# Value folds on quarters of the array, another order of GpSimd's splits, an unrolled quantised layer and another order of the third attention

## The reference

```python
# L0, L3: 16 heads of 64 columns
attn = softmax(mask(q @ k.T * scale))          # per head
out  = (attn @ v).reshape(b, n, INNER) @ Wo + bo
# L0 feed-forward: fake quantisation, one scale for the whole tensor
xq   = fake_quant(x)                           # needs max|x| of all blocks
h    = silu(xq @ q(w_gate).T) * (xq @ q(w_up).T)
y    = fake_quant(h) @ q(w_down).T             # needs max|h| of all blocks
# L2: one head of 256 columns, rows masked
out  = (softmax(where(mask, q @ k.T / 16, -1e10)) @ v) @ Wfc + bfc
# layers L1 to L3 follow it with mixtures of 8 experts
```

## Time and profile before

| what | value |
|---|---|
| median of 3 runs | 825.51 us (824.89 to 826.6) |
| profiled execution, own time | 823.46 us |
| its span in the trace | 821.7 us |
| mean granted clock of PE | 0.969 |
| busy share: PE, DVE, ACT, POOL | 91%, 69%, 53%, 42% |
| chain that ended last: PE, DVE, ACT, POOL | 59%, 9%, 8%, 8% |

### The profile page before, as it was taken

One profiled execution on the slowest core, in us unless ns is written; L12 is line 12 of the kernel. 1 busy time (PEld: TensorE's weight loads), 2 busy tenths in 40 slices (PEclk: granted clock), 3 DMA queues, 4 the chain that ended last, 5 costly groups with the idle time before them and its releaser, 6 DMA issues.

```text
span 821.7 us, 14453 instructions
## 1 busy us (share of the span) xinstructions
PE 750.0 (91%) x4384; PEld 604.9 (74%) x4384; DVE 568.0 (69%) x1647; ACT 438.5 (53%) x1182; POOL 348.2 (42%) x343
## 2 busy tenths in 40 slices
PE   6999989987799889799998879989999989899996
PEld 5677878863367666589996867756888876599984
DVE  3788878777988576657754878775667666855525
ACT  2477978857763753145553544445565244245542
POOL 1016998941301567614554011346541434324550
PEclk9999999997989978899999999999999999999999
DMA  8629970060001002248527400001000141334328
GB/s 275 102 91 345 327 244 1 1 205 0 1 1 39 2 20 89 100 126 269 161 85 259 132 0 2 2 0 39 1 1 1 51 151 56 104 111 149 123 85 307
DMA packets 55610, 83.38 MB, mean 101 GB/s; under 512 B 14816, under 2 KB 44512, under 8 KB 55264
## 3 DMA queue, kind: packets, MB, share of 16 engines
q1 hardware_dynamic: 48624, 63.52, 25.0%
q0 software_dynamic: 6912, 18.95, 6.4%
HBM read 61.41 MB, written 37.95 MB: 121 GB/s over the span
## 4 chain that ended last, share of the span: by engine, by line
PE 59%; DVE 9%; ACT 8%; POOL 8%; issue 6%; DMA 5%; DVEq 2%; POOLq 2%; SPq 1%; ACTq 0%
PE sh L848 16%; PE ob L848 13%; PE sh L1312 6%; PE ob L1312 6%; PE pt L805 6%; POOL xg L693 4%; PE pt L848 2%; POOL wA L630 2%; PE sh L1331 2%; PE pt L1304 2%; DMA work<-xg 2%; PE ob L1463 2%; DMA area<-yt 2%; ACT work L1560 1%; PE ob L1130 1%
## 5 line engine op out<-in xcount | busy, mean ns | idle before, releaser
L848 PE MATMUL ob<-area,work 128*128 128x256 f32 x512 | 116.1, 380 | 3.1 <-ACT work L1537 2.1
L702 POOL DMA_INDIRECT yt<-xn,work x72 | 69.3, 963 | 100.6 <-ACT xn L1872 86.1
L848 PEld LDWEIGHTS ob<-area,work 128*128 128x128 f32 x512 | 96.4, 190 | 19.8 <-issue 5.7
L607 POOL TENSOR_TENSOR rstd<-var,minush 128x4 f32<-128x4 f32 (+1 forms) x29 | 30.9, 1066 | 173.2 <-DVE var L2029 163.4
L1560 ACT ACTIVATE work<-work,mx 128x64 f32<-128x64 f32 x256 | 85.2, 335 | 19.4 <-DVE mx L2155 19.4
L693 POOL DMA_INDIRECT xg<-area,dest x64 | 63.5, 991 | 45.2 <-DVE dest L2492 27.5
L805 PE MATMUL pt<-ident,work 128*128 128x128 f32 (+1 forms) x292 | 41.4, 282 | 16.7 <-DMA cols<-in_L_xattn_ln_c_b 5.3
L805 PEld LDWEIGHTS pt<-ident,work 128*128 128x128 f32 (+1 forms) x292 | 33.4, 141 | 24.1 <-issue 14.3
L1537 ACT COPY work<-pt 128x512 f32<-128x512 f32 (+1 forms) x74 | 39.9, 582 | 17.7 <-PE pt L805 17.6
L848 PE MATMUL ob<-area 128*128 128x256 f32 (+1 forms) x152 | 40.2, 419 | 9.2 <-DVE x L2079 5.4
L1560 ACT ACTIVATION_READ_ACCUMULATOR work<-work,mx 128x1 f32 x256 | 48.1, 188 | 0.0
(11 more groups left out here) (364 smaller groups left out, 1933.9 us busy)
## 6 DMA issues: line engine op xcount, KB each, us to landing
work<-xg SPq DMA_DIRECT2D x80, 129.0 KB, 2.3
area<-in_L_ffn_w SPq DMA_DIRECT2D x4, 2048.0 KB, 10.9
area<-yt SPq DMA_DIRECT2D x16, 512.0 KB, 7.5
area<-in_L_xattn_Wq SPq DMA_DIRECT2D x2, 1024.0 KB, 10.1
x<-in_x SPq DMA_DIRECT2D x1, 2048.0 KB, 16.0
area<-in_L_xattn_Wo SPq DMA_DIRECT2D x2, 1024.0 KB, 11.5
area<-in_L_xattn_Wkv SPq DMA_DIRECT2D x2, 1024.0 KB, 6.3
out<-x SPq DMA_DIRECT2D x4, 512.0 KB, 4.4
```

Source lines behind the costliest of these rows:

```text
L607: pool.tensor_tensor(rstd[:, n], var[:, n], minush[:, n], ALU.pow).then_inc(given, 1)
L702: pool.indirect_dma_start(yt[:, :], bass.IndirectOffsetOnAxis(ap=back_to[:, 2 * i + q:2 * i + q + 1], axis=0), ypair[i][:, q * D:(q + 1) * ...
L848: mm = pe.matmul(o, a, b, start=(k == 0), stop=(k == len(lhs) - 1))
```

## The change

Four parts, in one kernel.

**A. Value folds.** The padded `vD16` and `vD6` become plain `vT16` and `vT6`: one copy of 512 columns takes the place of two of 64 rows, the clearing goes (two on DVE, one of 4096 columns on POOL in stage 4). `quarters` forms a step from eight matmuls of 64 rows and 64 columns: rows half `j` of the stationary, output partitions `64 * ((j + b) % 2)`, odd and even `b` in the two halves of `sh`. Both `j` of a `b` write the same columns of `sh` on different partitions. The keys' copies exchange the heads of a pair for odd batches to match. On DVE the first normalisation moves from after step 0 to after step 5, the bias from after step 3 to after step 7 (`bias_added`, for which PE waits before the first product with values), the statistics of block 3 into the attention. In stages 4 and 5 the fold units are dealt out anew, so that all eight value steps end in stage 4.

**B. Splits.** POOL does the split of `x` for block 2 behind the keys of block 2, ahead of the norm factors and the keys of block 3.

**C. Quantised layer.** The loop is written out. Gate and up of block 0 are interleaved with the transposes of blocks 2 and 3; twelve matmuls on `sh1` (`warm`) follow `largest`; the silu's table is loaded earlier; transposes 2 and 3 are moved by DVE after its groups 0 and 1; clearing and scales move ahead on DVE.

**D. Third attention.** DVE's order of `shift`, `norm1`, `combine` and `finish` changes, and `combine(3, 3)` is done in two parts; PE transposes the norm of the next block after the products with values, ACT moves it after the next block's exponentials.

```diff
+            def quarters(o, vT, w, m, b):
+
+                for j in range(2):
+                    r, to = slice(64 * j, 64 * j + 64), 64 * ((j + b) % 2)
+                    mm = pe.matmul(o[to:to + 64, b // 2 * D:(b // 2 + 1) * D], vT[r, m * NC_ + b * C:m * NC_ + (b + 1) * C],
+                                   w[r, m * D:(m + 1) * D], start=True, stop=True)
+                return mm
...
-                        mm = pe.matmul(sh[n % 2][:, b * D:(b + 1) * D], vD16[:, m, b, :, :].rearrange("p j c -> p (j c)"),
-                                       wo16[:, m * D:(m + 1) * D], start=True, stop=True)
+                        mm = quarters(sh[n % 2][:, b % 2 * 512:(b % 2 + 1) * 512], vT16, wo16, m, b)
...
-                        for j in range(2):
-                            ins = dve.tensor_copy(vD16[64 * j:64 * j + 64, 4 * e - 6:4 * e - 4, :, j, :],
-                                                  src[64 * j:64 * j + 64, :].rearrange("p (m b c) -> p m b c", m=2, b=NB))
-                        ins.then_inc(sh_taken, 1)
+                        dve.tensor_copy(vT16[:, (e - 2) * 1024 + 512:(e - 1) * 1024], src).then_inc(sh_taken, 1)
...
-                       12: lambda: normalise0(0), 13: lambda: first_stats(straight[2]), 14: lambda: norm0(1),
-                       15: values_bias, 16: lambda: first_stats(straight[3])})
+                       13: lambda: first_stats(straight[2]), 14: lambda: norm0(1),
+                       17: lambda: normalise0(0), 19: values_bias})
...
-        stage5_folds = ((26, 28, 30), (30, 34, 36), (36, 40, 42), (42, 44, 44))
+        stage4_folds = ((14, 16, 18), (18, 20, 22), (22, 24, 26), (26, 28, 28))
+        stage5_folds = ((28, 30, 32), (32, 34, 36), (36, 40, 42), (42, 44, 44))
...
             split_keys(2)
+            split_x(2)
+            block_rstd(NB - 1, NB - 1)
             split_keys(3)
...
+            warm(sh[1], 12)
...
+            turn(0)
+            turn(1)
+            pe.wait_ge(pt_moved, first_turn + 1)
+            gate_up(straight[0], 0)
+            turn(2)
+            gate_up(straight[0], 1)
+            turn(3)
+            gate_up(straight[0], 2)
+            pe.wait_ge(pt_moved, first_turn + NB)
+            for u in range(3, NB * NFQ):
+                gate_up(straight[u // NFQ], u % NFQ)
...
+                    combine(3, straight[-1], (0,))
+                    norm1(stage, straight[1])
+                    shift(straight[1])
+                    combine(3, straight[-1], (1,))
+                    shift(straight[2])
+                    norm1(stage, straight[2])
+                    finish(straight[0])
+                    shift(straight[3])
+                    finish(straight[1])
+                    norm1(stage, straight[3])
+                    finish(straight[2])
```

More of the change, by code:

```diff
@@ L1008, in fold_units @@
             def fold_units(first, last):
-                for u in range(first, min(last, KEYS6)):
+                for u in range(first, min(last, VALS6)):
                     o = sh[1][:, (u % 2) * 512:(u % 2 + 1) * 512]
@@ L1033, in fold_units @@
                             mm = pe.transpose(o[:, q * P:(q + 1) * P], wq16[:, at:at + P], ident[:, :])
-                    else:
-                        m, half = (u - 12) // 2, u % 2
-                        for q in range(2):
-                            mm = pe.matmul(o[:, q * D:(q + 1) * D], vD6[:, m, 2 * half + q, :, :].rearrange("p j c -> p (j c)"),
-                                           wo6[:, m * D:(m + 1) * D], start=True, stop=True)
-                    mm.then_inc(f_full, 1)
+                    mm.then_inc(f_full, 1)
+                for u in range(max(first, VALS6), min(last, KEYS6), 2):
+                    m = (u - VALS6) // 2
+                    pe.wait_ge(f_taken, u)
+                    if m == 0:
+                        pe.wait_ge(in_wo, 32)
+                    for b in range(NB):
+                        mm = quarters(sh[1][:, b % 2 * 512:(b % 2 + 1) * 512], vT6, wo6, m, b)
+                        if b >= 2:
+                            mm.then_inc(f_full, 1)
                 for u in range(max(first, KEYS6), last, 2):
@@ L1111, in attend1 @@
                             scores(straight[b.u + 1])
-                        norm_T1(stage, straight[b.u + 1])
+                        else:
+                            norm_T1(stage, straight[b.u + 1])
                     elif stage == 2:
@@ L1133, in attend1 @@
                         mm.then_inc(o_full, 1)
+                    if stage == 4 and b.u + 1 < NB:
+                        norm_T1(stage, straight[b.u + 1])
                     if stage == 2 and b.u == NB - 1:
@@ L1424, in _, with turn @@
             largest(0)
-            for b in range(NB):
+            warm(sh[1], 12)
+            first_turn = n
+            def turn(b):
+                n = first_turn + b
                 pe.wait_ge(x_int, b + 1)
@@ L1935, in gate_silu @@
                     if f in BY_POOL:
[L1936 removed]
+                        act.activation(hall[:, f, b.u * S:(b.u + 1) * S], gu[slot][1], ACT.Copy,
                                        scale=qw[:, 2, f:f + 1]).then_inc(gu_out, 1)
[L1938 removed]
+            for b in straight:
+                gate_silu(b)
             n = start_of("pt", 2) - 6
@@ L2085, in fold16 @@
                 g = gates[:, 0:1]
-                def off_diagonal(j):
-                    dve.memset(vD16[64 * j:64 * j + 64, :, :, 1 - j, :], 0.0)
-                if stage == 0:
-                    for j in range(2):
-                        off_diagonal(j)
                 for e in range(4):
@@ L2504, in bias_part, with combine @@
                 dve.tensor_copy(part, row).then_inc(bias_split, 1)
-            def combine(stage, b):
-                for h in range(2):
+            def combine(stage, b, parts=(0, 1)):
+                for h in parts:
                     dve.wait_ge(y_in[2 * b.u + h], 16 if stage == 3 else 32)
@@ new lines, in _ @@
+            for n in range(NB * NFQ):
+                b, f = straight[n // NFQ], n % NFQ
+                r = RFQ if f == NFQ - 1 else P
+                if f in BY_DVE:
+                    dve.wait_ge(act_done[1], b.scaled(NFQ, f + 1))
+                    dve.scalar_tensor_tensor(hall[0:r, f, b.u * S:(b.u + 1) * S], gu[n % 4][1][0:r, :],
+                                             qw[0:r, 2, f:f + 1], gate_t[n % 4][0:r, :],
+                                             ALU.mult, ALU.mult).then_inc(gu_half, 1)
+                if n in (0, 1):
+                    xq_move(2 + n)
+                if n >= 2 and n % 2 == 0:
+                    magnitude(n - 2)
```

183 lines of the change are left out of this document (72 added, 111 removed).

## The result

The changed kernel takes 816.85 us (median of 4 runs, 813.8 to 818.14), the kernel before beside it 826.06 (824.89 to 827.09): ratio 0.989, 95% interval 0.9861 to 0.9918. The forecast was 814 with a range of 809 to 820.5.

The account below looks back on a forecast made before the run. PE sets most of the end, but in the touched stretches others feed it, often DVE. Gains 5.3 + 1.0 + 2.0 + 2.4 + 1.0 = 11.7 off 823.46 give 811.8, on the median 814 us; range 809 to 820.5.

Parts of the forecast that it names:

- Value steps: Stage 0: quarter steps of 0.88 us, DVE stays the slow engine, scores start sooner; gain 5.3 us.
- The first rival: Value steps: quarters run two at a time, a step takes 1.75 us; 818.8 us on the median, chance 0.25.
- The fourth rival: Value steps: quarters do not run side by side, a step takes 3.5 us; slower at 835.3 us, chance 0.04.
- The second rival: PE's clock falls in the thinner value steps, half the scores run at half clock; 1.8 lost, 815.5 us, chance 0.10.
- First attention: Stage 0 attention: PE's 1.93 wait for POOL's split goes, moved statistics cost some; gain 1.0 us.
- Quantised layer: Third group's product comes sooner, DVE's 25.4 us behind it unchanged; gain 2.0, between 0.8 at half clock and 3.6.
- Third attention: DVE's new order removes idle times of 6.5 us and adds two waits totalling 4.15; gain 2.4 us.
- The walk along the waits: Third attention: following PE's work in the new order to find when DVE's two shifts can start; new waits 1.3 and 2.85.
- its waits of 1.3 and 2.85: Third attention: new DVE waits ahead of `shift` of block 2 (1.3 us) and of block 3 (2.85 us).
- the third rival: Third attention: DVE's new waits are as long as the old, 2.4 less gain; 816.2 us, chance 0.08.
- L2's experts: Stage 5: block 1's chain waits for two moves, 1.05 us, instead of four, 2.03; gain 1.0 us.
- The sum 11.7: Whole kernel: the five gains 5.3, 1.0, 2.0, 2.4 and 1.0 us added, taken off the profiled 823.46 us.

Follow-up runs that it names:

- the run with the clock held: Changed kernel, new third-attention order kept, plus matmuls that nothing reads on PE in that stage's waits: 814.61 us, ratio 0.9865.

## Why the prediction was right, and where it was wrong

**Value steps: right, to 0.1 us.** Steps of 0.88 were taken, 0.98 measured; DVE stayed the slow engine, and the four things taken off it add up (5.3 forecast, 5.22 measured), but for one wait of 0.56 for PE that the prediction had at nothing and some small gains that make up for it. The first rival, quarters in pairs, is out: a step would take 1.75. The Trainium skill, page "TensorEngine Tiling (Array Packing)", section "Restrictions and Gotchas", which stood behind that rival, does not agree with this trace if read as a rule that makes row halves wait: both row halves of a batch write one `sh` half on different partitions, and the steps ran at four quarters at a time. The fourth rival is out by the same row. The second rival, a fall of the clock in these steps, did occur in one execution, in the steps and not in the scores behind them where it had been priced (1.8 forecast, about 1.45 measured; a step went from 1.09 to 1.99).

**First attention: wrong.** Forecast 1.0, measured -0.11. The step that failed is that PE's wait of 1.93 was counted as path. It was a wait on a stretch where DVE was nearly as late as POOL: taking it away made PE's waits for DVE longer by 0.22 and 0.60 and the one for a norm that DVE gives by 0.64, and the order was worth 0.65. The moved statistics were priced about right (0.9 forecast, 0.76 measured).

**Quantised layer: the mechanism right, the size wrong.** Forecast 2.0 with 3.6 as the upper end, measured 4.84. The term was built on the clock: 0.8 at half, 3.6 at full. Without the twelve matmuls the clock fell and the layer took the same (36.44 against 36.42), because it was back before the second group, where in the kernel before the first two groups still ran at half (3.47). That the products among the transposes brought it back is likely, not shown. Two more things were missed: the third product came 4.2 sooner within the layer, more than the upper end of 3.6, and DVE's stretch behind it, held to be fixed at 25.4, took 24.76.

**Third attention: wrong in sign.** Forecast 2.4, measured -5.48. Two steps failed. The walk along the waits was made as if at full clock, and part of what it wanted to save, the wait of 0.73, was itself a fall of the clock: its waits of 1.3 and 2.85 came out as 0.80 and 3.49 in the run with the clock held, and a third of 1.55 before the last division was overlooked. So the gain at full clock is 0.7 against before and -0.5 against the old order with the short folds, and the third rival, that the order brings nothing, was nearer than the forecast. And the wait of PE for `ob`, which the walk had seen, was not asked for its effect on PE's clock, though the earlier trace rows showed a fall behind a wait of 2.2 in this very stage. The falls cost 6.2 us. The prediction had the clock as a rival, but in the value steps; the stage in which it had been seen to fall got none.

**L2's experts: right.** Forecast 1.0, measured 0.86. The further 1.63 behind them was in no term.

The sum 11.7 came out at 6.6 in the profiled executions and 9.2 in the medians: the 2.8 more in the quantised layer hid a third of the 7.9 less in the third attention, and 2.6 of the 9.2 are there because the kernel before was profiled in one of its shorter executions. That the time came out only 2.9 over the forecast is in part luck; without the 2.8 it would be 819.7, still inside the range.

## What to carry to other kernels

Before an order is changed, follow each wait that it makes on TensorE and price it twice: the wait itself, and the work behind it at half clock as a rival with a chance. Here the order cost the stage 6.7 us, of which 6.2 went when the waits were filled with matmuls that nothing reads; yet waits nearly as long (2.55, 1.83) passed without a fall in the old order, so the length of a wait alone does not tell. A wait that the trace shows is worth only what the next-latest engine leaves of it, so ask which engine comes next, and how late it is, if the wait goes. Where folds of block-diagonal operands are half zeros, quarters of the array without the zeros take some half of the time of the padded form (0.98 for 1.77 a step), in both orders of the quarters that were run.

## What the runs showed of the hardware

Four matmuls on 64 x 64 quarters run at once when the two of a pair write the same 256 columns of PSUM on different partitions: eight f32 ones with 256 columns in 0.98 us, 1.01 with neighbours on the same quarter.

The clock does not fall at the same places in each execution: the changed kernel's four runs spread over 4.3 us with mean granted clocks of 0.966 to 0.974, and the same value steps ran at 1.00 in one trace and at 0.52 in that of another kernel, whose code is the same up to there. The same wait of PE (2.28 and 2.27) was followed by a fall from 456.6 in one trace and by none in another.
